# Two-layer cross-attention kernel on one core: one string gives the order of an iteration's steps for every engine, and VectorE and GpSimd take the last stage's steps at the place where TensorE has them

## Chip, core and metric

One core of a Trainium2 chip (trn2). The metric is the device time of one execution in microseconds (us); lower is better. The kernel is written by hand, with its own semaphores, so the order of every engine's instructions is the order of the program.

## The reference, cut to what matters

Four sequences of 1024 rows of 256 values (x) pass through one transformer block and a further attention. All of it is float32.

```python
def block(x, ctx):                                   # 16 heads of 16 values
    h = attention(ln32(x, ln1), ln32(x, ln1), Wq1, Wkv1, Wo1) + bo1 + x        # self-attention over 1024 rows
    h = attention(ln32(h, ln2), ctx, Wq2, Wkv2, Wo2) + bo2 + h                 # cross-attention over 154 rows
    u = ln32(h, ln3) @ Wff1 + bff1                                             # 256 -> 2048
    lin, gate = split(u)
    return (lin * gate * sigmoid(1.702 * gate)) @ Wff2 + bff2 + h              # 1024 -> 256
# then: out = y + softmax((y Wq + bq) (ctx Wk + bk)^T) (ctx Wv + bv), one head, in layer 1
```

## The kernel before, in words

The 4096 rows are cut into 16 chunks of 256 rows. A software pipeline works on several chunks at once: iteration n does `pre` of chunk n (layer norm 1, Q, K and V), the running maxima of the self-attention scores, the self-attention of chunk n-5, `mid` of chunk n-6 (Wo, residual, layer norm 2, the second Q), `cross` of chunk n-7 (the cross-attention) and `last` of chunk n-8 (its Wo, layer norm 3, the feed-forward, the attention of layer 1, the output). Iterations 4 to 20 run so (`run`); `pre` is in iterations 4 to 15, `mid` from 6, `cross` from 7, `last` from 8, so that `last` is in 13 of them (8 to 20). What remains of the last three chunks is in `walk_end` (line 495), with an order of its own, the string END_ORDER.

An iteration has 32 slots (SLOTS), each of three places. `walk` (line 447) goes over slots and places and calls each engine's own work; every engine's block calls `walk` with its own functions, so that all engines have the same order of steps. The steps, with the letters that the change gives them:

- M: one score tile of the running maxima on TensorE (128x512, line 1705) and its reduction on VectorE (line 1383). There are two PSUM banks for it, so tile i needs the reduction of tile i-2. Q: the maxima of the pairs (VectorE, line 1387). T: their transpose (TensorE, line 1709) and the negated shift (VectorE, lines 1372 and 1374), which SyncE copies into qst.
- S: two scores of the self-attention (TensorE, line 1720), with the exponential (ScalarE, line 1152). V: the product with the values for two steps (line 1732). O: the copy of an attention result (ScalarE, line 1158).
- l: one of the 26 steps of `last`. On VectorE: step 2 multiplies oT2 by the inverse sums (line 1270), step 4 is the residual and its statistics (lines 1276, 1242, 1245), step 5 normalises (line 1249), step 6 makes the low part of y3 (line 1333), steps 7 to 14 are the hidden tiles hT 0 to 7 (lines 1339 and 1342), step 19 is a residual, 21, 22 and 24 are the maximum, the inverse sum and the output. On TensorE: step 3 is the Wo product, 6 a transpose, 7 to 14 are the ff1 products of tiles 0 to 7 (line 1649, 12 matmuls each, one bank, so tile m needs hT m-1), 15 to 18 are ff2 (line 1658). On ScalarE, step 6 gives the affine layer norm (line 1046) and the high part of y3 (line 1119), and steps 7 to 14 the tanh and the half gate (lines 1125 and 1127) which hT needs.
- c: one of the 36 steps of `cross`. Steps 1 to 12 are a maximum tile (TensorE, line 1585) and its reduction (VectorE, line 1307); step 13 is the transpose of the maxima (TensorE, line 1590), which needs all twelve reductions.
- m and p: the steps of `mid` (9) and `pre` (8). `mid` step 3 is, on VectorE, oT times the inverse sums (line 1270), and on TensorE the Wo product that needs it (line 1559, matmuls of line 1521); VectorE's step 4 is the residual with statistics and step 5 the normalisation. `pre` step 1 is VectorE's statistics, step 2 its normalisation.
- o, u, x, d, i, e, f: SyncE's stores and loads; VectorE has an inversion at i.

Where the steps of a chain fall is worked out by `share` (line 116) from how many steps there are, so that they are spread between a first and a last slot (PRE_AT, CROSS_AT, LAST_AT). `last` comes at place 1 of a slot on TensorE, ScalarE and SyncE (`advance(0, slot)`, line 483). VectorE and GpSimd call `walk` with `late_last=True`, and have it at the end of place 2, behind the slot's `mid` or `pre` step (line 487).

```python
                    if place == LAST_PLACE and not late_last:
                        advance(0, slot)
                    if place == SUB - 1:
                        advance(2, slot)
                        if late_last:
                            advance(0, slot)
```

Of the kernel before, what the change touches and what calls it, by code (L numbers as in the profile page):

```python
# [8 lines left out]
ALU = mybir.AluOpType  # L9
ACT = mybir.ActivationFunctionType  # L10
AX_X = mybir.AxisListType.X
# [104 lines left out]
def share(total, slot, at):  # L116


    if slot < at[0] or total == 0:
        return 0  # L120
    return 1 + min(total - 1, max(0, -(-(total - 1) * (slot + 1 - at[1]) // (at[2] - at[1]))))


def max_tiles(place):

    return min(2 * PAIRS, -(-(place + 1) * 2 * PAIRS // (MAX_LAST + 1)))


def max_unit(n, at):

    unit = HG * (n - ATT_LAG) + at // (SUB * KT) + LEAD
    return (unit if 0 <= unit < NU else None), at % (SUB * KT)


def xattn_kernel(nc, t, out):

    ctx = ExitStack()
    with ctx:
# [308 lines left out]
        def walk(n, flags, setup, pre, mid, cross, last, att_work, max_work, tail, loads=lambda slot: None,  # L447
                 late_last=False):


            has_pre, has_max, has_att, has_mid, has_cross, has_last = flags

            def pre_mid():
                work = mid(n - MID_LAG, has_pre) if has_mid else iter(())
                for _ in range(3 * has_mid):
                    next(work)
                    yield
                if has_pre:
                    yield from pre(n)
                yield from work  # L460

            chains = [
                (last(n - LAST_LAG) if has_last else iter(()), LAST_STEPS * has_last, LAST_AT),
                (cross(n - CROSS_LAG) if has_cross else iter(()), CROSS_STEPS * has_cross, CROSS_AT),
                (pre_mid(), PRE_STEPS * has_pre + MID_STEPS * has_mid, PRE_AT),
            ]

            def advance(i, slot, place=0, places=1):

                work, total, at = chains[i]  # L470
                at = [x * places for x in at]
                now = slot * places + place
                for _ in range(share(total, now - 1, at), share(total, now, at)):
                    next(work)

            for slot in range(SLOTS):
                for place in range(SUB):
                    if has_max:
                        max_work(SUB * slot + place)
                    if has_att:  # L480
                        att_work(slot, place)
                    if place == LAST_PLACE and not late_last:
                        advance(0, slot)
                    if place == SUB - 1:
                        advance(2, slot)
                        if late_last:
                            advance(0, slot)
                        for _ in range(setup_steps(n, slot)):
                            next(setup)
                        loads(slot)  # L490
                    advance(1, slot, place, SUB)
            tail()
            assert all(next(work, None) is None for work, _, _ in chains)
# [18 lines left out]
        def _(sp):  # L512
# [266 lines left out]
            def body(n, u, flags, att_before, after):  # L779
                has_max, has_att = flags[1:3]  # L780
                first = HG * (n - ATT_LAG)

                def max_work(at):
                    unit, place = max_unit(n, at)
                    if unit is not None and place == MAX_TURN:
                        sp.wait_ge(g_slo, unit + 1)
                        heads = slice(unit % HG * G, (unit % HG + 1) * G)
                        for row_, part in ((ROWS, sh_hi), (ROWS + 1, sh_lo)):
                            sp.dma_start(qst[row_:row_ + 1, heads, :].rearrange("a j (q p) -> a (j q) p", p=P),
                                         part[:, :]).then_inc(g_shl, 16)  # L790

                def loads(slot):

                    if after[4] and slot == CROSS_LOAD:
                        load_cross(n + 1 - CROSS_LAG)
                    g, at = divmod(slot, KT)
                    done = first + g - 1
                    if at == O_STORE and 0 <= done < NU and (has_att or att_before):
                        store_o(done)
                    if at == UNIT_LOAD and 0 <= done and done + HG < NU:  # L800
# [3 lines left out]
                    if after[5]:  # L804
                        for at, step in ((DEN_LOAD, load_last_den), (DEN_INV, store_last_inv),
                                         (LAST_LOAD, load_last), (SLOTS - 1, load_last_inv)):
                            if slot == at:
                                step(n + 1 - LAST_LAG)

                walk(n, flags, setup_work, pre, mid, cross, last, lambda slot, place: None, max_work, lambda: None, loads)  # L810
# [19 lines left out]
        def _(pool):  # L830
# [130 lines left out]
        def _(act):  # L961
# [185 lines left out]
            def body(n, u, flags, att_before, after):  # L1147
                def exp_tile(step, pair):
# [6 lines left out]
                def o_copy(unit):  # L1155
# [4 lines left out]
                def att_work(slot, place):  # L1160
                    step = SLOTS * (n - ATT_LAG) + slot
                    if place == 0:
                        exp_tile(step, 0)
                        exp_tile(step, 1)
                    if slot % KT == 0 and slot and place == SUB - 1:
                        o_copy(step // KT - 1)

                def tail():
                    if flags[2]:
                        o_copy(HG * (n - ATT_LAG + 1) - 1)  # L1170

                walk(n, flags, setup_work, pre_by(flags[3]), mid, cross_by(not flags[2]), last, att_work,
                     lambda at: None, tail)
# [8 lines left out]
        def _(dve):  # L1182
# [193 lines left out]
            def body(n, u, flags, att_before, after):  # L1376
                def max_work(at):
                    unit, place = max_unit(n, at)
# [14 lines left out]
                def inverses(slot):  # L1393
                    if after[5] and slot == DEN_INV:
                        invert(1, n + 1 - LAST_LAG)
# [391 lines left out]
```

## Time and profile before

| | |
|---|---|
| time, median of 3 runs | 1872.56 us (1865.7 to 1873.52) |
| the profiled execution | 1862.73 us, its span 1860.9 us |
| mean granted TensorE clock over the span | 0.967 |
| instructions | 33823 |
| iterations 8 to 15, from output to output (line 1365) | 108.1 us each (1073.36 to 1181.43 us) |
| iterations 16 to 20 | 103.1 us each |

The profile is of one execution. In a row of the timeline the first number is the start in us, the second the duration, and the brackets hold the idle time of that engine just before, with the instruction that ended it. Iteration 15 runs from 1076.2 to 1184.3 us, and its slot 7 begins at 1096.0 us. In the list of waits the numbers are the sum, how often, and the longest. In the busy times of a stretch each engine has its busy time and its instructions, and then comes the granted clock of TensorE (1.00 is 2.4 GHz, 0.50 is 1.2 GHz).

### The profile page before, as it was taken

The page shows a single profiled execution, that of the slowest core. Times are in us where ns is not written, and L with a number is a line of the kernel's source. Part 1 is how long each engine was busy: PE and PEld are TensorE (multiplying, and loading weights), DVE is VectorE, ACT ScalarE, POOL GpSimd, SP SyncE. Part 2 cuts the span into 40 slices and gives each one's busy share as a digit, 9 for nine tenths or more (in the row PEclk, how much of TensorE's full clock was granted, in tenths as well). Part 3 has the DMA queues.
Part 4 walks back from the last instruction along what each step waited for, and adds up shares of the span by engine and source line. Part 5 has one row for each costly group of instructions (what it writes and reads, how often), then busy time and mean ns, then how long its engine had stood idle before and what let it go on. Part 6 is the DMA issues. An engine that isn't in the chain of part 4 may idle for free.

```text
span 1860.9 us, 33823 instructions
## 1 busy us (share of the span) xinstructions
PE 1640.9 (88%) x12897; PEld 1037.2 (56%) x12897; DVE 1111.0 (60%) x2221; ACT 978.3 (53%) x2024; POOL 265.7 (14%) x344
## 2 busy tenths in 40 slices
PE   6799889898989989898998989899898989897877
PEld 5444444564646556564655656465555656464656
DVE  4556676747576575757656574756657575733332
ACT  3255656554656555565555545565554546554332
POOL 5210411201211020121102012100001010101110
PEclk9999999999999999999999999999999999998988
DMA  6904243335131412436121221335030220302200
GB/s 177 211 27 131 66 76 84 74 79 107 48 70 54 80 47 54 88 72 118 51 66 53 56 61 46 78 78 109 19 76 27 54 63 27 76 21 65 50 29 12
DMA packets 171647, 129.37 MB, mean 70 GB/s; under 512 B 40751, under 2 KB 161885, under 8 KB 171229
## 3 DMA queue, kind: packets, MB, share of 16 engines
q1 hardware_dynamic: 171421, 127.19, 29.2%
q8 instruction: 102, 1.67, 0.4%
q14 instruction: 60, 0.49, 0.1%
q10 hardware_dynamic: 64, 0.02, 0.0%
HBM read 78.92 MB, written 47.71 MB: 68 GB/s over the span
## 4 chain that ended last, share of the span: by engine, by line
PE 65%; DVE 21%; ACT 6%; issue 5%; DMA 2%; SPq 1%; ACTq 0%; POOL 0%; DVEq 0%; POOLq 0%
DVE mxh L1383 10%; PE ps_o L1732 10%; PE ps_last L1649 10%; PE ps_max L1705 9%; PE ps_s L1720 6%; PE ps_last L1658 6%; PE ps_pre L1513 4%; PE ps_cross L1617 3%; PE ps_pre L1521 3%; DVE mx L1307 3%; PE ps_cross L1603 2%; PE ps_last L1521 2%; ACT probs L1096 2%; PE ps_last L1687 2%; DVE hT L1342 1%
## 5 line engine op out<-in xcount | busy, mean ns | idle before, releaser
L1383 DVE TENSOR_REDUCE mxh<-ps_max 128x1 f32<-128x512 f32 x1024 | 667.8, 684 | 379.7 <-PE ps_max L1705 377.6
L1152 ACT ACTIVATE probs<-ps_s 128x512 f32<-128x512 f32 x1024 | 556.0, 598 | 316.3 <-PE ps_s L1720 310.7
L1705 PE MATMUL ps_max<-kst,qst 96*128 96x512 bf16 x1024 | 382.4, 390 | 86.1 <-DVE mxh L1383 71.0
L1720 PE MATMUL ps_s<-qst,kst 98*128 98x256 bf16 x2048 | 319.7, 278 | 1.2 <-ACT probs L1152 0.7
L1732 PE MATMUL ps_o<-probs,vg 128*17 128x256 f32 x4096 | 283.4, 393 | 6.4 <-ACT probs L1152 6.4
L1720 PEld LDWEIGHTS ps_s<-qst,kst 98*128 98x128 bf16 x2048 | 199.1, 99 | 92.2 <-issue 11.6
L1705 PEld LDWEIGHTS ps_max<-kst,qst 96*128 96x128 bf16 x1024 | 97.0, 97 | 229.2 <-DVE mxh L1383 170.2
L1096 ACT ACTIVATE probs<-ps_cross 77x512 f32<-77x512 f32 x224 | 133.5, 596 | 85.1 <-PE ps_cross L1603 85.1
L1732 PEld LDWEIGHTS ps_o<-probs,vg 128*17 128x17 f32 x4096 | 93.8, 98 | 136.6 <-issue 69.2
L1649 PE MATMUL ps_last<-y_hi,wff_hi 128*128 128x256 f32 x448 | 140.6, 314 | 24.5 <-DVE hT L1342 19.3
L1125 ACT ACTIVATE th<-ps_last,b_tanh 128x256 f32<-128x256 f32 x112 | 53.1, 474 | 160.4 <-PE ps_last L1649 160.4
L1339 DVE SCALAR_TENSOR_TENSOR th<-th,gb 128x256 f32<-128x256 f32 x128 | 59.8, 467 | 116.9 <-ACT gb L1127 116.3
L1649 PE MATMUL ps_last<-y_lo,wff_hi 128*128 128x256 f32 x448 | 127.5, 285 | 0.0
L1649 PE MATMUL ps_last<-y_hi,wff_lo 128*128 128x256 f32 x448 | 127.4, 284 | 0.0
L1658 PE MATMUL ps_last<-wff,hT 128*128 128x256 f32 x480 | 116.7, 388 | 5.3 <-DVE hT L1342 5.3
L1649 PEld LDWEIGHTS ps_last<-y_hi,wff_hi 128*128 128x128 f32 x448 | 85.8, 191 | 58.2 <-DVE hT L1342 34.8
L1603 PE MATMUL ps_cross<-q2st,k2st 98*77 98x256 bf16 x448 | 88.5, 279 | 20.5 <-ACT probs L1096 20.3
L1658 PEld LDWEIGHTS ps_last<-wff,hT 128*128 128x128 f32 x480 | 87.7, 190 | 33.1 <-issue 13.1
L892 POOL TENSOR_TENSOR qk_f<-qk_f,qk_parts 128x512 f32<-128x512 f32 x40 | 46.4, 1161 | 374.5 <-ACT qk_f L1085 220.4
L1649 PEld LDWEIGHTS ps_last<-y_lo,wff_hi 128*128 128x128 f32 x448 | 86.2, 192 | 0.6
L1649 PEld LDWEIGHTS ps_last<-y_hi,wff_lo 128*128 128x128 f32 x448 | 86.3, 193 | 0.0
L883 POOL TENSOR_SCALAR ve<-mv 128x2 f32<-128x2 f32 x34 | 7.8, 230 | 537.7 <-DVE mv L1245 537.7
(265 smaller groups left out, 2014.5 us busy)
## 6 DMA issues: line engine op xcount, KB each, us to landing
parts_s<-qk_parts SPq DMA_DIRECT2D x28, 384.0 KB, 3.1
o_s<-o_sb SPq DMA_DIRECT2D x64, 128.0 KB, 2.1
o_s<-o_sb SPq DMA_DIRECT2D x32, 256.0 KB, 2.2
oT<-o_s SPq DMA_DIRECT2D x62, 128.0 KB
den<-o_s SPq DMA_DIRECT2D x62, 128.0 KB
kst<-parts_s SPq DMA_DIRECT2D x16, 384.0 KB, 5.3
kst<-parts_s SPq DMA_DIRECT2D x48, 128.0 KB, 6.1
qst<-parts_s SPq DMA_DIRECT2D x64, 96.0 KB, 2.7
```

Of the source, the lines that this page charges most:

```text
L1096: nc.scalar.activation(probs2[:, h % PR2, :], cross_banks[spare][h % 2][0:CT, :], ACT.Exp, scale=SCALE).then_inc(c_e, 1)
L1152: nc.scalar.activation(probs[:, step % PR, 2 * pair:2 * pair + 2, :].rearrange("p j q -> p (j q)"), ps_s[pair][:, :], ACT.Exp, scale=SCALE ...
L1339: nc.vector.scalar_tensor_tensor(th[:, m % 2, :], th[:, m % 2, :], 1.0, gb[:, m % 2, :], ALU.add, ALU.mult).then_inc(c_gt, 1)
L1383: nc.vector.tensor_reduce(mxh[:, i // 2, i % 2:i % 2 + 1], ps_max[i % 2][:, :], AX_X, ALU.max).then_inc(g_mx, 1)
L1513: last = mm(bank[:, m * CH:(m + 1) * CH], w[:, k, m * P:(m + 1) * P], y[:, k, :], start=(k == 0), stop=(k == KD - 1))
L1521: last = mm(bank[:, i * D:(i + 1) * D], y[:, k, i * P:(i + 1) * P], w[:, k, :], start=(k == 0), stop=(k == KD - 1))
L1603: last = mm(cross_banks[spare][h % 2][0:CT, a * CH:(a + 1) * CH], k2st[:, at, a * CT:(a + 1) * CT], q2st[:, at, :], start=True, stop=True)
L1649: last = mm(last_banks(o)[m % 2][:, part * CH:(part + 1) * CH], wff1[w][:, k, cols_], y3[y][:, k, :], start=(i == 0), stop=(i == len(terms ...
L1658: last = mm(bank_[:, i * D:(i + 1) * D], hTs[e][:, m, i * P:(i + 1) * P], wff2[:, m, :], start=(m == 0), stop=(m == FM - 1))
L1705: mm(ps_max[i % 2][:, :], qst[0:ROWS, h, q * P:(q + 1) * P], kst[0:ROWS, h, k * 512:(k + 1) * 512], start=True, stop=True).then_inc(g_mt, 1)
L1720: last = mm(ps_s[pair][:, j * CH:(j + 1) * CH], kst[:, h, kt * P:(kt + 1) * P], qst[:, h, :], start=True, stop=True)
L1732: last = mm(ps_o[j * W:j * W + VW, 0:CH], vg[:, g, kt, j * VW:(j + 1) * VW], probs[:, step % PR, j, :], start=(kt == 0), stop=(kt == KT - ...
```

## The change

The constants of the places and `share`, `max_tiles` and `max_unit` by places are gone. A string ORDER has one letter per step, line by line a slot, and `walk` goes through it on every engine; where a chain doesn't run in an iteration, its letters do nothing.

```diff
-PRE_AT, CROSS_AT, LAST_AT = (1, 5, 22), (0, 0, 24), (1, 1, 32)
-CROSS_LOAD, DEN_LOAD, DEN_INV, LAST_LOAD = 26, 25, 27, 29
-SUB = 3
-PV_PLACE, LAST_PLACE = 1, 1
-MAX_LAST, MAX_PAIRED, MAX_TURN = 18, 19, 21
-O_STORE, UNIT_LOAD = 0, 2
+ORDER = (
+    "MSSccMMoc"
+    "MSSMllcMm"
+    "SScMVlMuc"
+    "MSSMlcM"
+    "SScMVlMc"
+    "MSSMlcMm"
+    "SScQVmc"
+    "TSSlcp"
+    "MSScMVlMOpoc"
+    "MSSMlcMp"
+    "SScMVlMpuc"
+    "MSSMcMp"
+    "SSMVlcMp"
+    "MSScMlMpc"
+    "SSQVlcp"
+    "TSSclmc"
+    "MSSMVcMOmo"
+    "MSScMlMmc"
+    "SSMVlcMmu"
+    "MSScMlMmc"
+    "SSMVlcMm"
+    "MSScMMc"
+    "SSQVlc"
+    "TSScl"
+    "MSSMVlMOo"
+    "MSSMlMd"
+    "SSMVMxu"
+    "MSSMlMi"
+    "SSMVlM"
+    "MSSMlMe"
+    "SSQVl"
+    "TSSfVO"
+)
...
-        def walk(n, flags, setup, pre, mid, cross, last, att_work, max_work, tail, loads=lambda slot: None,
-                 late_last=False):
+        def walk(n, flags, setup, pre, mid, cross, last, work):
...
+            chains = dict(
+                p=pre(n) if has_pre else None, m=mid(n - MID_LAG, has_pre) if has_mid else None,
+                c=cross(n - CROSS_LAG) if has_cross else None, l=last(n - LAST_LAG) if has_last else None)
+            seen = dict.fromkeys(ORDER, 0)
+            for letter in ORDER:
+                k = seen[letter]
+                seen[letter] += 1
+                if letter in work:
+                    work[letter](k)
+                elif letter in chains and chains[letter] is not None:
+                    next(chains[letter])
+                if letter == "S" and k % 2:
+                    for _ in range(setup_steps(n, k // 2)):
+                        next(setup)
...
-                walk(n, flags, setup_work, pre, mid, cross, last_by(1 - u), lambda slot, place: None, lambda at: None,
-                     lambda: None, late_last=True)
+                walk(n, flags, setup_work, pre, mid, cross, last_by(1 - u), {})
...
-                walk(n, flags, setup_work, pre, mid_by(1 - u, flags[5]), cross_by(not flags[2]), last,
-                     lambda slot, place: None, max_work, lambda: None, inverses, late_last=True)
+                walk(n, flags, setup_work, pre, mid_by(1 - u, flags[5]), cross_by(not flags[2]), last, dict(
+                    M=max_half, Q=max_pairs, T=max_turned, i=inverses))
```

The rest of the diff turns each engine's functions from slots and places to a count of their letter, with the same instructions and waits. Followed through, this is what it does to the order:

- TensorE, ScalarE and SyncE keep theirs in iterations 8 to 15.
- VectorE's order in the slots in question, in iterations 8 to 15 (S, V, O and SyncE's letters left out; i is VectorE's inversion):

| slot | before | after | step of `last` |
|---|---|---|---|
| 2 | c M M l c | c M l M c | 2 |
| 4 | c M M l c | c M l M c | 4 |
| 5 | M M c M m l | M M l c M m | 5 |
| 7 | T c p l | T l c p | 6 |
| 8 | M c M M p l c | M c M l M p c | 7 (hT 0) |
| 9 | M M c M p l | M M l c M p | 8 |
| 10 | c M M p l c | c M l M p c | 9 |
| 12 | M c M p l | M l c M p | 10 |
| 13 | M c M M p l c | M c M l M p c | 11 |
| 14 | Q c p l | Q l c p | 12 |
| 15 | T c m l c | T c l m c | 13 (hT 6) |
| 17 | M c M M m l c | M c M l M m c | 14 |
| 24, 25, 27, 29 | M M M l | M M l M | 20, 21, 22, 24 |

  The cross step of slot 7 is step 12, the last maximum; the first `c` of slot 8 is step 13. The `m` of slot 15 is `mid` step 3.
- GpSimd's steps of `last` move in the same way; those with work are 0, 4 and 5.
- Without `pre` (iterations 16 to 20), `mid`'s nine steps were in slots 1, 5, 7, 9, 11, 13, 15, 17 and 19 and are now in slots 1, 5, 6 and 15 to 20, on all engines. Without `mid` (iterations 4 and 5), `pre`'s eight steps were in slots 1, 5, 7, 9, 12, 14, 17 and 19 and are now in slots 7 to 14.
- The setup's steps (iterations 4 to 6) came at a slot's end and now come behind its second S.

## Rows read from the trace of the kernel before

**Rows 1.** The page: busy time, share of the span and instructions of each engine
```profile
PE 1640.9 (88%) x12897; PEld 1037.2 (56%) x12897; DVE 1111.0 (60%) x2221; ACT 978.3 (53%) x2024; POOL 265.7 (14%) x344
```
**Rows 2.** Waits of TensorE: us in total, times, longest
```profile
PE ps_max L1705 <- DVE mxh L1383: 71.0, 114, 2.2
...
PE ps_last L1649 <- DVE hT L1342: 19.3, 33, 1.4
...
PE ps_pre L1521 <- DVE oT L1270: 8.6, 7, 1.5
...
PE ps_last L1658 <- DVE hT L1342: 5.3, 9, 2.0
```
**Rows 3.** Timeline, slots 4 to 7 of iteration 15: start, us, engine, instruction
```profile
1088.87 0.69 DVE L1383 TENSOR_REDUCE mxh<-ps_max 128x1 f32<-128x512 f32 x1 [0.29 <-PE ps_max L1705]
...
1089.48 0.68 DVE L1276 TENSOR_TENSOR x<-ps_last,xb 128x512 f32<-128x512 f32 x1
...
1092.41 0.39 PE L1705 MATMUL ps_max<-kst,qst 96*128 96x512 bf16 x1 [2.20 <-DVE mxh L1383]
...
1094.27 1.04 DVE L1249 TENSOR_SCALAR oT<-x,mv,rs 128x256 f32<-128x256 f32 x2
...
1095.99 0.27 PE L1709 MATMUL ps_max<-ident,mxq 128*8 128x128 f32 x1 [1.25 <-DVE mxq L1387]
```
**Rows 4.** The same timeline, slots 7 and 8
```profile
1097.25 0.32 DVE L1307 TENSOR_REDUCE mx<-ps_pre 128x1 f32<-128x154 f32 x1 [0.26 <-PE ps_pre L1585]
...
1097.89 0.28 PE L1590 MATMUL ps_cross<-ident,mx 128*32 128x128 f32 x1
...
1098.31 1.06 PE L1732 MATMUL ps_o<-probs,vg 128*17 128x256 f32 x16
...
1099.20 0.69 DVE L1333 TENSOR_TENSOR y_lo<-den,y_hi 128x512 fp32r<-128x512 f32 x1 [1.63 <-ACT y_hi L1119]
...
1099.95 0.39 PE L1649 MATMUL ps_last<-y_hi,wff_hi 128*128 128x256 f32 x1 [0.58 <-DVE y_lo L1333]
```
**Rows 5.** The same timeline, slots 9 to 11
```profile
1104.43 0.39 PE L1649 MATMUL ps_last<-y_hi,wff_hi 128*128 128x256 f32 x1 [1.38 <-DVE hT L1342]
...
1107.99 0.73 DVE L1249 TENSOR_SCALAR pre_x<-pre_x,pre_mv,pre_rs 128x256 f32<-128x256 f32 x2
...
1111.68 0.69 DVE L1383 TENSOR_REDUCE mxh<-ps_max 128x1 f32<-128x512 f32 x1 [1.51 <-PE ps_max L1705]
...
1112.39 0.43 DVE L1339 SCALAR_TENSOR_TENSOR th<-th,gb 128x256 f32<-128x256 f32 x1
...
1112.80 0.38 PE L1705 MATMUL ps_max<-kst,qst 96*128 96x512 bf16 x1
```
**Rows 6.** The same timeline, slot 15
```profile
1132.52 0.67 DVE L1270 TENSOR_TENSOR oT<-oT,den 128x512 f32<-128x512 f32 x1
...
1133.67 1.89 PE L1521 MATMUL ps_pre<-wo,oT 128*128 128x256 f32 x8
...
1134.81 0.43 DVE L1339 SCALAR_TENSOR_TENSOR th<-th,gb 128x256 f32<-128x256 f32 x1 [1.62 <-ACT gb L1127]
...
1135.27 0.48 DVE L1342 SCALAR_TENSOR_TENSOR hT<-ps_last,cols,th 128x256 f32<-128x256 f32 x1
```
**Rows 7.** Timeline, slots 8 and 9 of iteration 16
```profile
1208.19 0.38 PE L1649 MATMUL ps_last<-y_hi,wff_hi 128*128 128x256 f32 x1 [0.39 <-DVE y_lo L1333]
...
1211.86 0.39 PE L1649 MATMUL ps_last<-y_hi,wff_hi 128*128 128x256 f32 x1 [0.57 <-DVE hT L1342]
...
1215.27 1.97 PE L1521 MATMUL ps_pre<-wo,oT 128*128 128x256 f32 x8 [1.47 <-DVE oT L1270]
```
**Rows 8.** Busy times by stretch: us, then by engine, PEclk, DMA share, GB/s
```profile
1106.00:1107.00 1.00, 1.00 (x6) 0.77 (x5) 0.00 (x0) 0.07 (x1) 0.00 (x0) 0.50 0.36 102
...
1090.20:1098.20 8.00, 4.55 (x45) 2.72 (x44) 7.03 (x18) 3.16 (x7) 3.76 (x6) 1.00 0.04 13
1198.30:1206.30 8.00, 5.61 (x42) 3.21 (x43) 7.02 (x18) 2.98 (x7) 3.77 (x6) 0.79 0.02 4
```

More of the change, by code:

```diff
@@ L113, in stages, with max_tile, max_unit @@
         0 <= n - lag < NCH for lag in (ATT_LAG, MID_LAG, CROSS_LAG, LAST_LAG))
[L116 to L132, printed above, removed]
+def max_tile(n, k):
+    unit = HG * (n - ATT_LAG) + k // (2 * PAIRS) + LEAD
+    return (unit if 0 <= unit < NU else None), k % (2 * PAIRS)
+def max_unit(n, k):
+    return max_tile(n, 2 * PAIRS * k)[0]
 def xattn_kernel(nc, t, out):
@@ L445, in run @@
                 body(n, n % 2, stages(n), stages(n - 1)[2], stages(n + 1))
-        def walk(n, flags, setup, pre, mid, cross, last, att_work, max_work, tail, loads=lambda slot: None,
-                 late_last=False):
+        def walk(n, flags, setup, pre, mid, cross, last, work):
             has_pre, has_max, has_att, has_mid, has_cross, has_last = flags
[L453 to L493, printed above, removed]
@@ L495, in walk_end @@
+            assert all(next(chain, None) is None for chain in chains.values() if chain is not None)
         def walk_end(mid, cross, last, loads=lambda letter: None):
@@ L779, in body, with store_shift, store_unit, load_unit @@
             def body(n, u, flags, att_before, after):
-                has_max, has_att = flags[1:3]
                 first = HG * (n - ATT_LAG)
[L783 to L800, printed above, removed]
+                def store_shift(k):
+                    unit = max_unit(n, k)
+                    if unit is None:
+                        return
+                    sp.wait_ge(g_slo, unit + 1)
+                    heads = slice(unit % HG * G, (unit % HG + 1) * G)
+                    for row_, part in ((ROWS, sh_hi), (ROWS + 1, sh_lo)):
+                        sp.dma_start(qst[row_:row_ + 1, heads, :].rearrange("a j (q p) -> a (j q) p", p=P),
+                                     part[:, :]).then_inc(g_shl, 16)
+                def store_unit(k):
+                    if 0 <= first + k - 1 < NU and (flags[2] or att_before):
+                        store_o(first + k - 1)
+                def load_unit(k):
+                    done = first + k - 1
+                    if 0 <= done and done + HG < NU:
                         load_stack(done + HG)
@@ L803, in loads, with load_next_cross, for_last, load @@
                             load_values((done // HG + 1) // CPB, done % HG)
[L804 to L810, printed above, removed]
+                def load_next_cross(k):
+                    if after[4]:
+                        load_cross(n + 1 - CROSS_LAG)
+                def for_last(step):
+                    def load(k):
+                        if after[5]:
+                            step(n + 1 - LAST_LAG)
+                    return load
+                walk(n, flags, setup_work, pre, mid, cross, last, dict(
+                    T=store_shift, o=store_unit, u=load_unit, x=load_next_cross, d=for_last(load_last_den),
+                    i=for_last(store_last_inv), e=for_last(load_last), f=for_last(load_last_inv)))
             def end_loads(letter):
@@ L1147, in body, with exp_tile @@
             def body(n, u, flags, att_before, after):
-                def exp_tile(step, pair):
+                def exp_tile(k):
+                    if not flags[2]:
+                        return
+                    step, pair = SLOTS * (n - ATT_LAG) + k // 2, k % 2
                     act.wait_ge(g_s, 2 * step + pair + 1)
@@ L1158, in o_copy @@
                     nc.scalar.copy(o_sb[:, unit % 2, :], ps_o[:, 0:CH]).then_inc(g_o, 1)
[L1160 to L1173, printed above, removed]
+                walk(n, flags, setup_work, pre_by(flags[3]), mid, cross_by(not flags[2]), last, dict(
+                    S=exp_tile, O=o_copy))
             head()
@@ L1693, in body, with max_scores @@
             def body(n, u, flags, att_before, after):
-                def max_work(at):
-                    unit, place = max_unit(n, at)
+                def max_scores(k):
+                    unit, i = max_tile(n, k)
                     if unit is None:
@@ L1722, in scores, with values_of @@
                     last.then_inc(g_s, 1)
-                def values(step):
+                def values_of(step):
                     unit, kt = divmod(step, KT)
```

90 lines of the change are left out of this document (48 added, 42 removed).

## The prediction

> **What bounds the kernel now.** I read the busy times first: TensorE works 1640.9 of 1860.9 us, VectorE 1111.0 [rows 1]. So the time is TensorE's work plus its idle gaps, and a change of order can only move the gaps. The time stays the same if nothing that TensorE waits for moves. Then the list of TensorE's waits: the largest are for VectorE, namely reductions of the running maximum, the hidden tile hT of the feed-forward, and the normalised attention output oT [rows 2]. Then the timeline of iteration 15 (from 1076.2 to 1184.3 us), which stands for iterations 8 to 15, and that of iteration 16, which stands for 16 to 20. TensorE's, ScalarE's and SyncE's order within a slot is left as it was (iterations 8 to 15), so everything hangs on VectorE, where each step of `last` moves ahead of whatever came between TensorE's `l` and the end of the slot: a reduction, a cross step, a step of `mid` or `pre`. The question at each of the 26 steps is what that work was needed for, and what the moved step waits for. VectorE takes its work in program order, so if the moved step waits, ready work behind it waits too.
>
> **Part 1, steps without work or without consequence: 0 us.** Steps 0, 1, 3, 15 to 18, 20, 23 and 25 hold no VectorE work, and step 19 keeps its place. Step 2 (slot 2) swaps with one reduction, whose consumer in slot 3 comes just ahead of the product that needs step 2; both are needed before that product. Steps 21, 22 and 24 each swap with one reduction of about 0.6 us, and TensorE needs the pair. GpSimd's only moved work is two additions against two others in slot 5, both used ten slots later or more, so ten slots cover them; without that cover they would cost the 1.4 us by which the later one slips.
>
> **Part 2, slots 4 and 5: -0.3 us.** Step 4 (residual, statistics) now starts when slot 4's first reduction ends, at 1088.5 and not at 1089.48; the 0.29 us in which VectorE waited for the next maximum tile goes, and some of the overlap of starts. TensorE waits 2.20 us in slot 5 and 1.25 us for the transposed maximum in slot 7 [rows 3]; it now waits in three pieces, but the turn of slot 7 comes only 0.3 us earlier (0.2 to 0.5), because VectorE is full here. Step 5 keeps GpSimd's additions beside it, so I keep its 1.04 us for two operations [rows 3], against 0.73 us for the like pair in slot 9 [rows 5].
> The Trainium skill (Advanced Engine Details and Errata, VectorE Performance Modes) says that GpSimd and VectorE's two-port instructions block each other on a shared port. If step 5 were to slip clear of the additions, it would save 0.31 us in each of 13 iterations, 4 us; by the rows it does not.
>
> **Part 3, slots 7 and 8: +1.55 us, net +1.25 us.** Step 6 is the low part of y3. It waited 1.63 us for ScalarE, and the last cross maximum (0.32 us at 1097.25) was done ahead of it; TensorE's transpose of the cross maxima went at 1097.89, then a maximum tile and the value products of 1.06 us, so that ff1 of tile 0 had only 0.58 us to wait [rows 4]. Now the last cross maximum stands behind step 6. Step 6 ends near 1099.8 (0.3 earlier with part 2: 1099.5), the cross maximum at 1099.75, the transpose goes at 1099.85 after 2.5 us of idle time, the tile and the value products follow (0.12 + 0.22 + 0.99), and ff1 starts at 1101.2, not 1099.95. Bounds: +1.0 (a quicker hand-over) to +1.6 (no gain from part 2).
>
> **Part 4, slots 9 and 11: +0.75 us.** TensorE's second maximum tile of an odd slot needs the reduction of the slot before that now stands behind hT. In slot 11 it went at 1112.80 with its reduction at 1111.68 [rows 5]; now hT (12.39 to 13.34) is first, the reduction ends near 1113.95, and the tile goes 1.2 us late. Of that, 0.55 us falls on a wait for a cross exponential that is there anyway: +0.65. In slot 9 hT 0 gains about 0.8 us, because `pre`'s statistics no longer stand ahead of it, and loses it to the same reduction: the distance from ff1 tile 0 to tile 1 was 4.48 us [rows 4, 5] and becomes about 4.6, +0.1. Bounds for both together: -0.5 to +1.5.
>
> **Part 5, slot 15: +2.78 us.** This is the largest term. `mid` step 3 on VectorE is oT times the inverse sums; it ran at 1132.52, ahead of hT 6, and so was ready when TensorE ended ff1 of tile 6 and took the Wo product at 1133.67. Now it stands behind hT 6, which waits for the tanh and gate of that same ff1 and ran from 1134.81 to 1135.75 [rows 6]. So oT is ready at 1135.75 + 0.6 and TensorE goes on at 1136.45. 1136.45 - 1133.67 = 2.78 us, with nothing else that TensorE may do meanwhile: its next letters stand behind the Wo product. Bounds: 2.2 to 3.0.
>
> **Part 6, slots 17 and 18: -0.42 us.** Here the move helps. hT 7 no longer stands behind the 0.73 us of `mid`'s normalisation, and the wait of ff2 (5.3 us in 9 waits [rows 2]) goes, 0.42 us in this iteration. Sum for iterations 8 to 15: -0.3 + 1.55 + 0.75 + 2.78 - 0.42 = 4.36 us, eight times: 35 us.
>
> **Part 7, iterations 16 to 20, without `pre`.** Parts 2, 3 and 5 hold (+4.03). `mid`'s nine steps were spread, with Wo in slot 9, where it waited 1.47 us for oT [rows 7]; it is now in slot 15, and this wait goes: -1.47. The chain from ff1 to ff1 was 3.67 us (1208.19 to 1211.86 [rows 7]), set by hT. In slots 9 and 13 a reduction and a tile are now added to it (about +0.9 each), and in slot 11 +0.4. Sum 4.03 - 1.47 + 2.2 = 4.8 us, five times: 24 us.
>
> **Part 8, the start.** In iterations 4 and 5 `pre` has fixed slots 7 to 14 (it was 1 to 19), and setup steps stand behind the scores, not at the slot's end. On VectorE 12 of them can now keep a ready reduction waiting, up to 0.5 us each; earlier filling can win as much. I take 0, within 4 us both ways. The last three sub-chunks are walked by another string that doesn't change: 0.
>
> **Part 9, the clock.** TensorE's granted clock is at half (1.2 GHz) in short stretches, after gaps: 0.50 at 1106, just after the 1.38 us wait of slot 9 [rows 5, 8]. After the 2.20 us gap of slot 5 it fell in iteration 16 (0.79 over 8 us) but not in 15 (1.00) [rows 8]: 0.21 x 2 x 8 = 3.4 us at half speed, which costs about half of its busy part, 1.6 us. The change makes two new gaps of 2.5 and 2.8 us in each iteration. Nearest are the gaps of slot 5, of like length, followed by a fall in some iterations. I take one more low stretch per iteration, 13 x 1.6 = 21 us; bounds 0 and two (42 us).
>
> **Sum.** 35 + 24 + 21 = 80 us. The profiled execution took 1862.7 us (span 1860.9), so it would take 1943. The median shown is 1872.6, 9.8 above it; with it the forecast is 1872.6 + 80, about 1952 us. Of three runs two are near the median, so I say 1950.
>
> **The rivals.**
> (a) The waits come but the clock does not fall more often: 1872.6 + 59 = 1932 us. For it: iteration 15 kept full clock after 2.20 us. Against: iteration 16.
> (b) Only one of the two big stalls is real or the other is absorbed later, for instance by VectorE's own backlog in slots 0 to 6: without part 5, 13 x 2.8 = 36 us less and one low stretch fewer, 1895 us. Against it: TensorE's gaps behind slot 15 are all measured from its own steps, so they shift with it.
> (c) Faster: hT ready earlier is what decides. The place is ff1 and ff2 in slots 8 to 18; the prices are the waits for hT, 19.3 and 5.3 us, and for oT, 8.6 us [rows 2], with some 10 us of low clock behind them: 1872.6 - 43 = 1830 us. It decides only if steps 6 and 13 do not hold up the cross maximum and oT, that is if ScalarE had finished before VectorE got there. The 1.63 and 1.62 us that VectorE waited at those very steps [rows 4, 6] speak against it.
> (d) No change: VectorE's new order costs TensorE as much as it gives, 1872 us. It would need parts 3 and 5 to be hidden; TensorE has no other work there.
> (e) Two more low stretches per iteration: 1972 us.
>
> **Chances.** Forecast 0.50, (a) 0.20, (b) 0.10, (e) 0.10, (c) 0.05, (d) 0.05. About 0.5% is what a measurement of this kernel can tell from no change. Faster by over 0.5% 0.05, within it 0.05, slower 0.90. The range takes in (a) and (e) with the bounds of parts 3 to 5 (together about 1 us per iteration either way): 1908 to 1984 us.
>
> **What would show it.** TensorE's busy time stays near 1641 at full clock and grows only by low clock; the waits of the Wo product for oT (L1270) rise from 8.6 to about 13 x 2.7 = 35 us; the transpose of the cross maxima (L1590) newly waits about 2.5 us in 13 iterations for the cross maximum (L1307); the wait of ff2 for hT nearly goes; the period of iterations 8 to 15 goes from 108.1 to 112.4 us or, with the clock, 114. Wrong would be: a period at or below 108 us, or oT ready before ff1 of tile 6 ends.

## The result, and the profile after

The changed kernel took 1951.66 us (median of 3 runs, 1949.85 to 1961.34) against 1872.56 before: ratio 1.0447, 95% interval [1.0396, 1.0497], 79 us slower. The profiled execution took 1949.85 us (span 1948.1). On the page of the changed kernel, the line that answers to [rows 1]:

```profile
PE 1668.8 (86%) x12897; PEld 1055.8 (54%) x12897; DVE 1109.7 (57%) x2221; ACT 980.6 (50%) x2024; POOL 265.9 (14%) x344
```

TensorE does the same 12897 matmuls and is busy 27.9 us longer; VectorE's and GpSimd's busy times stay. So of the 87.2 us by which the span grew, 27.9 are matmuls that ran slower and 59.3 are idle time. By iteration (from one output of the chain `last` to the next) the idle time of TensorE went from 9.8 to 13.9 us in iterations 8 to 15 and from 10.3 to 15.6 in 16 to 20, together 130.0 to 189.6 us; before iteration 8 and after iteration 20 it is the same within 0.4 us. The period of iterations 9 to 15 went from 107.7 to 113.7 us on average. (Before the change it is 108.2 and 107.2 us by turns; the 108.1 of the table above is that of iteration 15.) The waits of TensorE in the changed kernel, to be held against [rows 2] (us in total, times, longest):

```profile
PE ps_max L1699 <- DVE mxh L1370: 106.1, 166, 2.0
PE ps_pre L1516 <- DVE oT L1258: 36.0, 15, 2.7
PE ps_cross L1585 <- DVE mx L1295: 28.3, 14, 2.1
...
PE ps_last L1644 <- DVE hT L1330: 3.7, 16, 0.5
...
PE ps_last L1653 <- DVE hT L1330: 2.3, 2, 2.0
```

The waits for hT went from 19.3 and 5.3 to 3.7 and 2.3 us: that is what an earlier `last` gives. Three others took their place: oT 8.6 to 36.0, the cross maxima from none of note to 28.3, the running maximum 71.0 to 106.1. The timeline of the changed kernel shows where, in iteration 15 (start, us, engine, instruction):

```profile
1132.33 0.39 PE L1699 MATMUL ps_max<-kst,qst 96*128 96x512 bf16 x1 [1.19 <-DVE mxh L1370]
...
1133.47 0.39 PE L1699 MATMUL ps_max<-kst,qst 96*128 96x512 bf16 x1 [0.55 <-DVE mxh L1370]
...
1140.41 0.69 DVE L1321 TENSOR_TENSOR y_lo<-den,y_hi 128x512 fp32r<-128x512 f32 x1 [1.87 <-ACT y_hi L1113]
1141.02 0.31 DVE L1295 TENSOR_REDUCE mx<-ps_pre 128x1 f32<-128x154 f32 x1
...
1141.39 0.29 PE L1585 MATMUL ps_cross<-ident,mx 128*32 128x128 f32 x1 [1.93 <-DVE mx L1295]
...
1147.07 0.39 PE L1699 MATMUL ps_max<-kst,qst 96*128 96x512 bf16 x1 [1.69 <-DVE mxh L1370]
...
1178.18 0.43 DVE L1327 SCALAR_TENSOR_TENSOR th<-th,gb 128x256 f32<-128x256 f32 x1 [2.22 <-ACT gb L1121]
1178.64 0.48 DVE L1330 SCALAR_TENSOR_TENSOR hT<-ps_last,cols,th 128x256 f32<-128x256 f32 x1
1179.04 0.68 DVE L1258 TENSOR_TENSOR oT<-oT,den 128x512 f32<-128x512 f32 x1
1179.87 1.32 PE L1516 MATMUL ps_pre<-wo,oT 128*128 128x256 f32 x5 [2.67 <-DVE oT L1258]
```

Read in groups: slot 5 has its wait in pieces (1.19, 0.55). In slot 7 VectorE sits 1.87 us in front of y_lo, waiting for ScalarE, with the cross maximum of 0.31 us behind it and TensorE behind that. In slot 15 it is the same with 2.22 us in front of th, then hT, then oT, and TensorE 2.67 us late; in [rows 6] oT was done before th.

The granted clock just before and after the gaps of slot 5 (columns as in [rows 8]; the clock is the third number from the end):

```profile
1125.00:1133.00 8.00, 6.36 (x52) 3.86 (x49) 7.39 (x17) 3.26 (x6) 1.13 (x3) 1.00 0.20 55
1133.00:1141.00 8.00, 5.76 (x42) 3.20 (x42) 5.73 (x13) 4.32 (x9) 2.66 (x4) 0.79 0.09 25
```

0.21 x 2 x 8 = 3.4 us at half clock. Taking the clock microsecond by microsecond from 318 us to the end of iteration 20, the kernel before has 19 stretches of 3.4 us at half clock (or neighbours that add up to them), the changed one 38. None of the 38 is in iteration 8; 28 begin in slots 5 to 9 of iterations 9 to 20 (two or three in each), four behind slot 11 in iterations 16 to 19, and six behind slot 15. In this part TensorE's busy time grew from 1247.1 to 1273.6 us, 26.5 us for 19 stretches, 1.4 us each.

### The profile page after: what moved, and what is told of

The parts are those of the page before. It is cut to its first block, busy times and chain, and to the rows that moved or that the text cites. A ratio compares the mean times of both kernels' runs of the same rounds, so it can differ in the third digit from the quotient of the medians.

```text
span 1948.1 us, 33823 instructions
## 1 busy us (share of the span) xinstructions
PE 1668.8 (86%) x12897; PEld 1055.8 (54%) x12897; DVE 1109.7 (57%) x2221; ACT 980.6 (50%) x2024; POOL 265.9 (14%) x344
## 4 chain that ended last, share of the span: by engine, by line
PE 64%; DVE 23%; ACT 6%; issue 4%; DMA 1%; SPq 1%; POOL 0%; DVEq 0%; ACTq 0%; POOLq 0%
DVE mxh L1370 11%; PE ps_o L1733 11%; PE ps_last L1644 10%; PE ps_max L1699 9%; PE ps_s L1721 6%; PE ps_last L1653 6%; PE ps_pre L1508 4%; DVE mx L1295 3%; PE ps_pre L1516 3%; PE ps_cross L1612 3%; PE ps_cross L1598 2%; ACT gb L1121 2%; DVE hT L1330 2%; PE ps_last L1682 1%; DVE th L1327 1%
## 5 line engine op out<-in xcount | busy, mean ns | idle before, releaser
L1699 PE MATMUL ps_max<-kst,qst 96*128 96x512 bf16 x1024 | 384.9, 394 | 119.8 <-DVE mxh L1370 106.1
L1733 PE MATMUL ps_o<-probs,vg 128*17 128x256 f32 x4096 | 292.0, 402 | 6.4 <-ACT probs L1149 6.4
L1644 PE MATMUL ps_last<-y_hi,wff_hi 128*128 128x256 f32 x448 | 149.1, 333 | 3.7 <-DVE hT L1330 3.7
L1644 PE MATMUL ps_last<-y_lo,wff_hi 128*128 128x256 f32 x448 | 133.3, 298 | 0.0
L1644 PE MATMUL ps_last<-y_hi,wff_lo 128*128 128x256 f32 x448 | 132.6, 296 | 0.0
L1644 PEld LDWEIGHTS ps_last<-y_hi,wff_hi 128*128 128x128 f32 x448 | 91.9, 205 | 35.4 <-issue 24.0
L1644 PEld LDWEIGHTS ps_last<-y_lo,wff_hi 128*128 128x128 f32 x448 | 92.7, 207 | 1.1
L1644 PEld LDWEIGHTS ps_last<-y_hi,wff_lo 128*128 128x128 f32 x448 | 92.4, 206 | 0.0
```

The lines of the kernel that those rows point to most:

```text
L1644: last = mm(last_banks(o)[m % 2][:, part * CH:(part + 1) * CH], wff1[w][:, k, cols_], y3[y][:, k, :], start=(i == 0), stop=(i == len(terms ...
L1699: mm(ps_max[i % 2][:, :], qst[0:ROWS, h, q * P:(q + 1) * P], kst[0:ROWS, h, k * 512:(k + 1) * 512], start=True, stop=True).then_inc(g_mt, 1)
L1733: last = mm(ps_o[j * W:j * W + VW, 0:CH], vg[:, g, kt, j * VW:(j + 1) * VW], probs[:, step % PR, j, :], start=(kt == 0), stop=(kt == KT - ...
```

## The experiments

Eleven kernels. They differ from the changed kernel in the strings alone (and one in added matmuls): `walk` takes the string as an argument, VectorE and, where said, GpSimd get their own, TensorE, ScalarE and SyncE keep ORDER. Idle time and low stretches are given for the part from 318 us to the end of iteration 20; the changed kernel has 189.6 us and 38, the kernel before 130.0 and 19. Each ratio is to the kernel before, run on the same chip: its median was 1867.90 us beside e1 to e4, 1870.59 beside e5 to e8 and 1871.71 beside e9 to e11.

This part doesn't hold the whole difference. Behind iteration 20 every kernel has the same order (END_ORDER) and 37 to 39 us of idle time of TensorE, but TensorE is at half clock there for 39 us in the kernel before, 43 in the changed kernel and 53 to 70 in the versions below. In e8, where it is 70 us, the end takes 9.4 us longer than in the kernel before, which gives back part of the 31.6 us gained up to there. Why the end is slower in these versions is open.

**e1_slot15, e2_slot7, e3_slots7_15: the two large stalls.** On VectorE alone, the step of `last` goes back to the place that it had, in slot 15, in slot 7, in both.

```diff
-    "TSSlcp"
+    "TSScpl"
...
-    "TSSclmc"
+    "TSScmlc"
```

> The changed kernel with one pair put back on VectorE alone: in slot 15 the multiplication of oT by the inverse sums (step 3 of mid) stands ahead of hT 6 again. Theory (VectorE's program order makes TensorE wait at the Wo product): TensorE's waits for oT (36.0 us) fall under 5 us, the period of iterations 8 to 15 falls by 2.7 us, and with the low-clock stretches that follow this gap the time falls by 35 to 45 us, to about 1908 us, 1.02 of the kernel before. Rival (the gap only moves, since later waits absorb it): under 10 us less, above 1940 us.

> The changed kernel with the other pair put back on VectorE alone: in slot 7 the last cross maximum stands ahead of the low part of y3 again. Theory: the transpose of the cross maxima no longer waits (28.3 us), the first ff1 waits a little for y3 instead, and the time falls by 1.25 to 1.6 us in each of 13 iterations plus 5 to 15 us of low clock: about 1923 us, 1.027 of the kernel before. Rival (y3 is the bound, so this transpose was in its shadow): no change within 5 us of 1951.

> Both pairs put back on VectorE, all the other steps of the last stage still amid the slot. Theory: the two add up, 53 us of idle time and most of the 19 added low-clock stretches go, about 1878 us, 1.003 of the kernel before (1.00 to 1.01); what is left is the reductions behind hT in slots 9, 11 and 13. Rival (many small swaps matter as much as the two): above 1900 us.

Slot 15 alone: 1898.49 us, ratio 1.0162 [1.0142, 1.0182]; idle 158.8 us, 24 low stretches. Slot 7 alone: 1914.37 us, 1.0247 [1.0211, 1.0283]; idle 170.2, 26 stretches. Both: 1869.94 us, 1.0009 [0.999, 1.0028]; idle 143.3, 10 stretches. Each takes its own wait away and leaves the other. The waits of TensorE with slot 15 restored (for oT 1.3 us are left, none of them in iterations 8 to 20):

```profile
PE ps_max L1734 <- DVE mxh L1405: 104.2, 164, 2.0
PE ps_cross L1620 <- DVE mx L1330: 29.3, 14, 2.1
```

and with slot 7 restored:

```profile
PE ps_max L1734 <- DVE mxh L1405: 107.2, 168, 2.1
PE ps_pre L1551 <- DVE oT L1293: 36.0, 15, 2.7
```

So putting back two of the 26 steps takes the whole loss away: 82 us by the medians. In the two profiled executions this part is 88 us shorter, of which idle time makes 46 (189.6 to 143.3) and busy time 42 (1273.6 to 1232.0 us), with 28 fewer low stretches. The clock part is larger than I had given it: with both stalls gone there are fewer low stretches than in the kernel before, 10 against 19.

**e4_all_late: all steps of `last` back.** VectorE and GpSimd both get every `l` at its old place; what is left of the change is the new places of `mid`, `pre` and setup.

```diff
-    "MSSMllcMm"
+    "MSSMcMmll"
...
-    "MSScMVlMOpoc"
+    "MSScMVMOploc"
-    "MSSMlcMp"
+    "MSSMcMpl"
```

> All of VectorE's and GpSimd's steps of the last stage put back behind the slot's mid or pre step; what is left of the change is the fixed places of mid in iterations 16 to 20 and of pre in 4 and 5, and the setup's steps behind the scores. Theory: nothing of the loss is in these; 1860 to 1875 us, 0.995 to 1.002 of the kernel before, with iterations 16 to 20 shorter by up to 1.5 us each, since the Wo product of slot 9 no longer waits for oT. Rival (the places of mid and pre or the setup cost time of their own): 5 us or more above the kernel before, in iterations 4 to 7 or 16 to 20.

1859.68 us, ratio 0.9954 [0.9939, 0.9969]; idle 126.4 us, 16 stretches. The waits for hT are back:

```profile
PE ps_max L1768 <- DVE mxh L1439: 70.8, 117, 2.2
...
PE ps_last L1713 <- DVE hT L1399: 19.5, 34, 1.4
...
PE ps_last L1722 <- DVE hT L1399: 7.3, 14, 2.0
```

The rest of the change is worth 0.5%: in iterations 16 to 20 the wait of the Wo product for oT in slot 9 (1.47 us in [rows 7]) is gone.

**e5_pool_late: GpSimd alone.** Its strings go back as in e4, VectorE keeps ORDER.

> The changed kernel, with only GpSimd's steps of the last stage put back behind the slot's other work. My theory: GpSimd's part of the change costs nothing and gives nothing, since all of the time lies in VectorE's order: no difference from the changed kernel, about 1951 us, ratio 1.045 to the kernel before, TensorE's idle time of iterations 8 to 20 near 190 us. Rival: GpSimd's additions, earlier now, hold the port that VectorE's fast forms want, and that is part of the loss: 1945 us or less.

1958.55 us, ratio 1.0463 [1.0432, 1.0494], against 1.0447 [1.0396, 1.0497] of the changed kernel: GpSimd's own order costs and gives nothing that can be told from these times. Why it doesn't is not shown. The execution that was profiled took 3920.56 us (it isn't in the ratio), with matmuls at about twice their time (785 ns for a maximum tile, 389 in the changed kernel), so its idle times can't be compared; in it GpSimd's additions don't lie beside VectorE's step 5, whose two operations took 0.40 us each.

**e6_filled: the gap of slot 15 filled.**

```diff
+                    for i in range(10):
+                        mm(ps_pre[:, 0:CH], ident[:, :], wo1[:, 0, :], start=True, stop=True)
                     pe.wait_ge(c_on[0], o + 1)
```

> The changed kernel, with ten matmuls of no use (identity by a weight tile, into the bank that the next product clears) put ahead of TensorE's wait for oT in slot 15, so that this gap of 2.7 us is mostly filled; the output is as before. Theory 'gaps bring the half clock': the low stretches that follow slot 15 (6 of the 38 between 318 us and the end of iteration 20) go and perhaps a few others, about 9 us less than the changed kernel, 1942 us, with idle time some 29 us less and busy time some 20 us more. Rival 'the half clock does not come from this gap': low stretches stay at 38 and the time at about 1951 us. If the ten matmuls take longer than the gap, the time rises by that, up to 0.3 us in each of 13 iterations.

1976.48 us, ratio 1.0557 [1.0529, 1.0585]. The size of my filler was wrong: the ten fp32 matmuls are 20 records of 0.22 us each, 4.4 us for a gap of 2.67, so each Wo product of the 13 iterations with this gap comes 1.7 us later, and the three others, which had 0.89, 0.39 and 0 us of wait, up to 4.4 us: 34 us. The question is answered all the same. The wait for oT at these products and the six stretches behind slot 15 are gone, and 28 of 38 are left in all. The Wo products themselves, in the changed kernel and then in the filled one (duration ns min/median/max):

```profile
L1516 PE MATMUL ps_pre<-wo,oT x128: 379/379/702, 207.6 to 1805.6; 128*128 128x256 f32 x128
```

```profile
L1516 PE MATMUL ps_pre<-wo,oT x128: 379/379/379, 212.0 to 1831.3; 128*128 128x256 f32 x128
```

The same products behind a gap are slow in some iterations, up to 702 ns, and behind other matmuls never. So this gap does bring the half clock. The times fit roughly: e5, the changed kernel in all but GpSimd, ran at 1958.6 on the same chip, and 1958.6 + 34 - 10 x 1.4 = 1979.

**e7_ahead_of_mp: behind the reductions, but ahead of `mid` and `pre`.** Both engines; slots 7 and 15 as in e3.

```diff
-    "MSScMVMOploc"
-    "MSSMcMpl"
+    "MSScMVMOlpoc"
+    "MSSMcMlp"
```

(against e4; the same kind of swap in the other slots in which `l` stood behind `m` or `p`).

> The last stage's steps behind the slot's last reduction, as in the kernel before, but ahead of the steps of mid and pre, on VectorE and GpSimd both; slots 7 and 15 with the last stage's step last of all on VectorE's side as before. Compared with the version that had every step at its old late place (1859.7 us, waits for hT 19.5 and 7.3 us): theory 'hT is late only because mid and pre stand ahead of it': the waits for hT fall to about 10 and 3 us and the time to about 1852 us, ratio 0.991. Rival 'what hT gains the transposed maxima or the turned x lose': 1860 us, ratio 0.995, with another wait larger by as much.

1844.99 us, ratio 0.9856 [0.9834, 0.9877]; idle 115.0 us, 15 stretches. The waits of TensorE:

```profile
PE ps_max L1768 <- DVE mxh L1439: 70.2, 114, 2.2
...
PE ps_last L1713 <- DVE hT L1399: 11.1, 29, 0.6
...
PE ps_last L1722 <- DVE hT L1399: 2.3, 2, 2.0
```

hT's waits fall from 26.8 to 13.4 us and the wait for the running maximum stays at 70. So the purpose of the change, hT earlier, is sound; what hT must not pass are the reductions and the cross maxima.

**e8_even_behind: e3 with slots 8, 10 and 12 as well.** GpSimd too.

```diff
-    "MSScMVlMOpoc"
+    "MSScMVMOlpoc"
...
-    "SScMVlMpuc"
+    "SScMVMlpuc"
...
-    "SSMVlcMp"
+    "SSMVcMlp"
```

> The version with slots 7 and 15 restored (1869.9 us; idle 143.3 us, 10 low stretches in iterations 8 to 20), with the last stage's step of slots 8, 10 and 12 also behind the third reduction but ahead of pre's step. Theory: what is left of the loss is that a reduction stands behind hT and TensorE's next maximum tile waits for it: the idle time of iterations 16 to 20 falls by about 1.5 us each and that of 8 to 15 by 0.3, some 10 us in all: 1860 us, ratio 0.996. Rival: the loss of slots 9 and 11 alone (odd slots, untouched here) is what counts, and the time stays within 3 us of 1870.

1835.93 us, ratio 0.9806 [0.978, 0.9833]; idle 116.8 us, 6 stretches. More than three times what I expected (34 us under e3, or 38 by the ratios, not 10). I had counted with the odd slots, but the reduction that TensorE lacks in slot 9 belongs to slot 8. Slots 8 and 9 of iteration 14 in e3:

```profile
994.80 0.42 DVE L1362 SCALAR_TENSOR_TENSOR th<-th,gb 128x256 f32<-128x256 f32 x1 [1.01 <-ACT gb L1156]
...
995.26 0.48 DVE L1365 SCALAR_TENSOR_TENSOR hT<-ps_last,cols,th 128x256 f32<-128x256 f32 x1
...
995.66 0.68 DVE L1405 TENSOR_REDUCE mxh<-ps_max 128x1 f32<-128x512 f32 x1
...
996.39 0.39 PE L1734 MATMUL ps_max<-kst,qst 96*128 96x512 bf16 x1 [1.69 <-DVE mxh L1405]
```

and in e8:

```profile
982.93 0.69 DVE L1439 TENSOR_REDUCE mxh<-ps_max 128x1 f32<-128x512 f32 x1 [0.32 <-PE ps_max L1768]
...
983.63 0.43 DVE L1396 SCALAR_TENSOR_TENSOR th<-th,gb 128x256 f32<-128x256 f32 x1
983.67 0.39 PE L1768 MATMUL ps_max<-kst,qst 96*128 96x512 bf16 x1
...
984.10 0.48 DVE L1399 SCALAR_TENSOR_TENSOR hT<-ps_last,cols,th 128x256 f32<-128x256 f32 x1
...
984.64 0.38 PE L1713 MATMUL ps_last<-y_hi,wff_hi 128*128 128x256 f32 x1 [0.57 <-DVE hT L1399]
```

In e3 VectorE waits 1.01 us for ScalarE with a ready reduction behind it. In e8 the reduction fills that time, th starts without a wait, and TensorE's 1.69 becomes 0.57 us.

**e10_slot8: slot 8 of these alone.** The first of the three edits above, on e3.

> The version with slots 7 and 15 restored (1869.9 us), with one more letter moved: the last stage's step of slot 8 (the first hidden tile) behind the third reduction, ahead of pre's step. Theory: of the 34 us between that version and the one with slots 8, 10 and 12 moved, slot 8 carries the largest part, since TensorE's wait for the reduction in slot 9 is 1.69 us in each of 13 iterations and brings low stretches behind it: 13 x 1.1 us plus some 5 us of low clock, about 1851 us. Rival 'the next step of the chain gives it back': 1865 us or more, because slot 11's tile then waits longer for its reduction.

1846.91 us, ratio 0.9863 [0.9841, 0.9886]; idle 132.1 us, 4 stretches. Slot 8 carries 23 of the 34 us (27 of 38 by the ratios). In iteration 14 the gap of slot 9 is gone and that of slot 11 stays at 1.03 us; it goes with slots 10 and 12, in e8.

**e9_unsplit: the gap of slot 5 in one piece again.** e8 with slots 1 to 5 in the order of the kernel before, except that in slots 1 and 5 the step of `last` stays ahead of that of `mid`, as in e7.

```diff
-    "SScMVlMc"
-    "MSSMlcMm"
+    "SScMVMlc"
+    "MSSMcMlm"
```

> The best version so far (slots 7 and 15 restored, slots 8, 10 and 12 with the last stage's step behind the third reduction; 1835.9 us, 6 low stretches in iterations 8 to 20), with slots 1 to 5 in the order of the kernel before, so that TensorE's gap of slot 5 is one of 2.2 us again and not pieces of 0.4, 1.2 and 0.55. Theory 'half clock follows the length of a single gap, not the idle time': idle time stays within 5 us of 116.8, low stretches in iterations 8 to 20 rise from 6 to about 14, and the time rises by about 8 x 1.6 = 13 us to 1849 us. Rival 'the clock falls whatever the gap's shape, the difference between the versions came from elsewhere': 6 or so low stretches stay and the time is 1836 us.

1846.81 us, ratio 0.9859 [0.9837, 0.9882], 10.9 us above e8. The pieces of e8 in iteration 14:

```profile
965.54 0.39 PE L1768 MATMUL ps_max<-kst,qst 96*128 96x512 bf16 x1 [0.37 <-DVE mxh L1439]
972.16 0.39 PE L1768 MATMUL ps_max<-kst,qst 96*128 96x512 bf16 x1 [1.19 <-DVE mxh L1439]
973.31 0.61 PE L1768 MATMUL ps_max<-kst,qst 96*128 96x512 bf16 x1 [0.55 <-DVE mxh L1439]
```

and the one of e9:

```profile
971.85 0.61 PE L1768 MATMUL ps_max<-kst,qst 96*128 96x512 bf16 x1 [2.20 <-DVE mxh L1439]
```

Idle time is the same (115.8 against 116.8 us), the low stretches go from 6 to 15, and all of them, in both, lie at the gap of slot 5. Iterations 9 to 20 take 1245.0 against 1235.4 us. The spans of the two profiled executions are nearly equal all the same (1839.6 and 1838.7 us), since elsewhere e9 had less half clock: 17.1 against 30.7 us up to the output of iteration 8, which comes 5 us earlier, and 62.9 against 70.2 us behind iteration 20, which takes 3.6 us less. Over all executions the mean granted clock was 0.965 to 0.972 in e8 and 0.958 to 0.964 in e9, so the 10.9 us are a difference in clock.

That pieces bring less half clock than one gap is shown for this pair alone. The same three pieces stand in slot 5 of the changed kernel and of e2, and half clock begins right at them in nine of 13 iterations in the one and in ten in the other; both have further gaps, of 1.7 us in slot 9 and 2.7 us in slot 15.

**e11_step5_late: VectorE's step of slot 5 in slot 6.** VectorE alone, on e8.

```diff
-    "MSSMlcMm"
-    "SScQVmc"
+    "MSSMcMm"
+    "SScQlVmc"
```

> The best version so far (1835.9 us), with VectorE's step 5 of the last stage (the two additions of slot 5) taken out of slot 5 and done in slot 6, ahead of the reduction over the pairs, where VectorE has less to do. Theory 'VectorE's work in slots 4 and 5 makes the gaps of slot 5': TensorE's waits of 1.2 and 0.55 us in slot 5 shrink by together 0.5 to 1 us, 13 times, and the transposed maximum of slot 7 waits no longer than before: about 1826 us. Rival 'the work only moves, and the chain over all reductions to slot 7 is what counts': the gap appears in slot 7 instead, 1836 us or a little more.

1826.11 us, ratio 0.9755 [0.9732, 0.9778]: the best version, 2.4% faster than the kernel before; idle 106.4 us, 8 stretches. The time came as expected, but not by the waits that I had named: 1.19 and 0.55 us stand in slot 5 as before. Nor is the edit quite what I had described: its letter stands behind Q, so the step comes behind the reduction over the pairs and not ahead of it. What falls most is the wait for the transposed maximum in slot 7, from 11.7 to 5.3 us in all (e8, then e11):

```profile
PE ps_max L1776 <- DVE mxq L1447: 11.7, 23, 1.0
```

```profile
PE ps_max L1776 <- DVE mxq L1447: 5.3, 20, 1.0
```

In e8, slots 5 and 6 of iteration 14:

```profile
972.16 0.39 PE L1768 MATMUL ps_max<-kst,qst 96*128 96x512 bf16 x1 [1.19 <-DVE mxh L1439]
...
973.76 1.14 DVE L1306 TENSOR_SCALAR oT<-x,mv,rs 128x256 f32<-128x256 f32 x2
973.97 1.51 POOL L977 TENSOR_TENSOR x<-x,bo 128x256 f32<-128x256 f32 x2
...
976.72 0.15 DVE L1447 TENSOR_REDUCE mxq<-mxh 128x8 f32<-128x16 f32 x1
```

and in e11:

```profile
967.08 0.39 PE L1768 MATMUL ps_max<-kst,qst 96*128 96x512 bf16 x1 [1.19 <-DVE mxh L1439]
...
968.88 1.41 POOL L977 TENSOR_TENSOR x<-x,bo 128x256 f32<-128x256 f32 x2
...
970.58 0.15 DVE L1447 TENSOR_REDUCE mxq<-mxh 128x8 f32<-128x16 f32 x1
970.64 0.73 DVE L1306 TENSOR_SCALAR oT<-x,mv,rs 128x256 f32<-128x256 f32 x2
```

From slot 5's gap to the reduction over the pairs it is 3.50 us and no longer 4.56: the step of 1.14 us no longer stands ahead of that reduction. And the step itself, once clear of GpSimd's additions, takes 0.73 and not 1.14 us, while the additions take 1.41 against 1.51. All of it is in the second of the step's two operations, about 0.82 us beside the additions and 0.41 clear of them; the first takes 0.40 us in both, though GpSimd works beside it in e8 too. The step is the normalisation of the row by `mv` and `rs`, which the expectation wrongly called additions. The prediction put this at 0.31 us in each of 13 iterations if step 5 slipped clear of the additions, and rightly didn't count it, since in the changed kernel it does not; moved here, it is 0.41 us. The Trainium skill (Advanced Engine Details and Errata, VectorE Performance Modes) says that GpSimd's instructions and those of VectorE that use two ports interfere with or block each other, since they share a port. The traces agree for the second operation and show nothing of it for the first; that the port is the cause is the page's statement, the runs show the durations alone.

## Why the prediction was right

1950 us was forecast and 1951.7 measured, for the reason given. That the two are so near is in part luck. Between the profiled executions, from which the terms were worked out, the sum was 80 us and the measured difference 87.2: 1943 us was forecast for the one after and 1949.85 came, the rest being the clock. The medians are only 79 us apart, since the profiled execution before was 9.8 us under its median and the one after was the fastest of three. The steps, each against iteration 14 (before and after; 8.81 and 12.88 us of waits) and, for part 7, iteration 16:

- **Part 2, slots 4 and 5 (-0.3):** 2.20 us became 0.37 + 1.19 + 0.55, -0.1. The turn of slot 7 had no wait to lose in this iteration. In iteration 15, from which the rows of the prediction are, it had 1.25 us and lost them, so the waits grew by only 3.28 us there (9.60 to 12.88). Right in kind, and small.
- **Part 3, slots 7 and 8 (+1.55):** the transpose of the cross maxima waits 1.93 us and ff1's wait of 0.39 goes: +1.54. The wait itself was given as 2.5 and its knock-on as less than it; the sum was right.
- **Part 4, slots 9 and 11 (+0.75):** the waits for hT (1.38 + 0.42) and for the cross exponential (0.55) became reductions' waits of 1.69 and 1.03: +0.37. Half of what I took, inside its bounds.
- **Part 5, slot 15 (+2.78):** 2.67 us, in each of the 13 iterations (the other 1.3 us of the wait for oT are in iterations 6 and 7). e1 shows its full price: 53 us with the clock, of which idle time is 31.
- **Part 6, slot 18 (-0.42):** exactly so. The sum for this iteration is +4.07 in place of 4.36, and iterations 8 to 15 have 4.1 us more idle time each on average.
- **Part 7, iterations 16 to 20 (+4.8):** measured +5.3 on average. In iteration 16: slot 7 +1.65, slot 9 for hT +1.12, Wo in slot 9 -1.47, slot 11 +0.71, slot 13 +0.76, slot 15 +2.67. The chain of hT was given +2.2 and measured +2.6.
- **Part 8, the start (0):** within 0.1 us of idle time.
- **Part 9, the clock (+21 from 13 stretches):** +26.5 from 19. The number was too low, the price of each (1.6) a little too high at 1.4. The stretches came in slots 5 to 9 and behind slot 11 rather than behind the two new gaps alone; behind slot 15 there are six, not thirteen.

The idle time, 59 us forecast, is 59.6: the terms that were off by some tenths, up and down, cancel. The lower end of the range, 1908 us, doesn't follow from its bounds: 1932 less about 1 us in each of 13 iterations is 1919. Rival (a), waits without a clock, fell by the 27 us of busy time, and (b) by the idle sums. Rival (e), 26 more stretches, is about as far from the 19 measured as the forecast of 13. Rival (c) was right that hT's waits go, and e7 shows that they can be had (13 us of them); it failed on the condition that I had named, ScalarE being late at steps 6 and 13: VectorE waits 1.87 and 2.22 us there. What I did not see is that the order between the two was open: I took the choice to be between hT early and hT late.

## What to carry to other kernels

On an engine that takes its work in order, before moving a step forward, look at whether it sits waiting when its turn comes: its own early start is worth nothing, and ready short work behind it pays the wait. Put ready work whose consumer is the bottleneck (here the reductions) ahead of the step that waits for another engine, and put the waiting step ahead of work that nobody needs soon (here `pre` and `mid`): orders by these two rules turned +4.5% into -1.9% (e8) with nothing but letters, and the move of step 5 behind the reduction over the pairs, again ready work for the bottleneck first, made it -2.4% (e11). About 0.5% of that is owed to the new places of `mid` (e4). Count the clock too: here 26.5 us of half clock came on top of 59.6 us of stalls.

## What the runs showed of the hardware that was not expected

- The shape of TensorE's idle time can matter for its clock, not only the sum. With equal idle time, one gap of 2.20 us in slot 5 came with 15 stretches of half clock, and 0.37 + 1.19 + 0.55 us in its place with 6 (e9, e8). It is no rule: the same pieces came with half clock in nine iterations of 13 in the changed kernel, and in ten in e2.
- One gap of 2.67 us was followed by half clock in six iterations of 13, and in none when filled with matmuls of no use (after, e6).
- More idle time doesn't mean more half clock: e10 has 132.1 us of idle time and 4 stretches, e7 115.0 us and 15.
- VectorE's normalisation of 128x256 twice takes 1.14 us beside GpSimd's additions and 0.73 us clear of them, all by the second operation (0.82 and 0.41 us); its reductions out of TensorE's banks 0.66 to 0.69 us in both places (e8, e11).
- The same last stretch of the program had TensorE at half clock for 39 us in one kernel and for 70 us in another, with 39 and 37 us of idle time (before, e8).
